# Selective-scan layer with routed experts: packed small TensorE products, a reordered chunk border, and fewer C products on VectorE

## Time and profile before

| | us |
|---|---|
| median of 3 runs | 815.91 |
| lowest and highest | 810.96 and 816.17 |
| the profiled execution's own time | 810.87 |
| its span, first to last instruction | 808.9 |
| mean granted TensorE clock (1 is full) | 0.939 |
| PE, DVE, POOL, ACT busy | 717.3, 525.1, 514.4, 482.0 |

### The profile page before, as it was taken

One profiled execution on the slowest core, in us unless ns is written; L12 is line 12 of the kernel. 1 busy time (PEld: TensorE's weight loads), 2 busy tenths in 40 slices (PEclk: granted clock), 3 DMA queues, 4 the chain that ended last, 5 costly groups with the idle time before them and its releaser, 6 DMA issues. The chain is left out here.

```text
span 808.9 us, 17785 instructions
## 1 busy us (share of the span) xinstructions
PE 717.3 (89%) x5898; PEld 626.9 (78%) x5899; DVE 525.1 (65%) x901; ACT 482.0 (60%) x977; POOL 514.4 (64%) x641
## 2 busy tenths in 40 slices
PE   7689899899998997898898875969999999999993
PEld 6567778677777776777676875958999999999992
DVE  4778989988889899779699973353333343333430
ACT  3579899899898986877886662412322333223320
POOL 1499789788887996998998763642333443334420
PEclk9589999999999997989999987979999999999997
DMA  9677843253243433634555659421111111111000
GB/s 217 179 227 260 285 131 108 90 133 105 79 133 105 118 92 82 113 76 107 113 92 62 170 157 259 37 19 62 56 43 60 38 40 53 42 55 50 25 8 1
DMA packets 45768, 82.58 MB, mean 102 GB/s; under 512 B 7800, under 2 KB 16253, under 8 KB 45696
## 3 DMA queue, kind: packets, MB, share of 16 engines
q1 hardware_dynamic: 39680, 69.05, 32.1%
q0 software_dynamic: 6016, 12.61, 6.3%
HBM read 70.48 MB, written 13.91 MB: 104 GB/s over the span
## 5 line engine op out<-in xcount | busy, mean ns | idle before, releaser
L618 POOL TENSOR_TENSOR w_sb<-w_sb,Csb 128x512 f32<-128x512 f32 x218 | 275.9, 1275 | 56.1 <-DVE w_sb L1151 53.6
L1151 DVE TENSOR_TENSOR_SCAN w_sb<-WW,hlast,w_sb 128x512 f32<-128x512 f32 x164 | 202.3, 1268 | 26.9 <-PE WW L974 19.7
L855 ACT ACTIVATE dt<-WW,b1c 128x128 f32<-128x128 f32 x312 | 89.1, 370 | 194.1 <-PE WW L1050 184.4
L959 PEld LDWEIGHTS WW<-b_sb,xin 64*128 64x128 f32 x2048 | 133.7, 198 | 76.0 <-issue 50.1
L959 PE MATMUL WW<-b_sb,xin 64*128 64x130 f32 (+1 forms) x2048 | 159.0, 297 | 37.4 <-DVE w_sb L1151 22.9
L784 ACT ACTIVATE w_sb<-dt,negA 128x512 f32<-128x512 f32 x256 | 170.1, 709 | 12.7 <-DVE dt L1180 7.4
L1066 PE MATMUL misc<-w_sb,dt 128*128 x624 | 144.1, 385 | 8.7 <-issue 8.3
L990 PE MATMUL YY<-sm,w_sb 128*128 128x128 f32 x1024 | 146.3, 290 | 0.0
L678 POOL DMA_INDIRECT y_out<-CbX,ocol x39 | 44.7, 1147 | 153.9 <-DVE CbX L1462 153.6
L1066 PEld LDWEIGHTS misc<-w_sb,dt 128*128 128x128 f32 x624 | 117.8, 194 | 24.1 <-issue 9.2
L990 PEld LDWEIGHTS YY<-sm,w_sb 128*128 128x128 f32 x1024 | 129.7, 160 | 0.0
(11 more groups left out here) (213 smaller groups left out, 821.9 us busy)
## 6 DMA issues: line engine op xcount, KB each, us to landing
w_sb<-c_rows SPq DMA_DIRECT2D x86, 256.0 KB
CbX<-c_rows SPq DMA_DIRECT2D x42, 256.0 KB, 3.9
w_sb<-w_in SPq DMA_DIRECT2D x20, 512.0 KB, 5.9
token_rows<-row SPq DMA_DIRECT2D x16, 512.0 KB
w_sb<-w_in SPq DMA_DIRECT2D x24, 256.0 KB
xin<-x_in SPq DMA_DIRECT2D x16, 256.0 KB, 4.1
w_sb<-x_in SPq DMA_DIRECT2D x14, 256.0 KB, 9.4
b_sb<-b_in SPq DMA_DIRECT2D x1, 780.0 KB, 6.4
```

The costliest lines, as they stand in the source:

```text
L618: eng.tensor_tensor(by_time(hc[g % NHC]), in_tiles(hb_of(g)), in_tiles(Csb[i % NCS][:, :]), ALU.mult).then_inc(s_hcp, 1)
L855: g = eng.activation(hT[u % 2][:, j * P:(j + 1) * P], hps[u % 2][:, j * P:(j + 1) * P], ACT.Gelu, bias=b1c[u][:, j:j + 1])
L959: return eng.matmul(to[:, at:at + width], x_rows[rows, k, h * P:(h + 1) * P], band[rows, k, at % P:at % P + width], start=(k == 0), stop=( ...
L1151: eng.tensor_tensor_scan(hb_of(g) if pooled(g) else w_of(g), w_of(g), A[g % NA], hlast[(q - 1) % 2][:, h * N + n:h * N + n + 1] if q % NC ...
```

## The change

- `VECTOR_UNITS`: (4, 10) in chunk 0, (8,) in chunks 1 to 6, (1, 5, 9, 13) in chunk 7. Seven pairs of items, 14 items, move from VectorE to GpSimd and ScalarE (19 pairs before, 12 after).
- cbt becomes one transpose of all four row tiles, spread over partition groups of 32 (CS = 32), instead of four; the four products of u read those groups, two at step 13 (`u_a`) and two at 14; its table is repeated in the four groups (made from a transpose of `invA4` and one VectorE instruction in the opening, ahead of the first `dt_add`, in place of two ScalarE copies).
- route becomes `routeT`: eight products with the 32-wide padded Wr stationary, each row tile into its own group of 32 PSUM partitions, then an evacuation (ScalarE) and one transpose a step later.
- bcd is split over two steps; xn0 and xn1 come one step earlier, vlast goes from 15 to 10, `row_products` from GpSimd's step 14 to 9.
- At the border (n = 0, 1) `add_y` comes ahead of `make_w`; `finish_rows`, `ln2_stats` and `aggregate` come one item earlier; `dt_add` and `u_times_x` move by one item or less.
- `choose(1)` and rank of chunks 4 to 6 leave chunk 7 and go behind the last scan; the routing of chunk 7 is done ahead of `outputs(0)`; `choose(2)` goes to tile 0, `place_tokens(2)` to tile 1; twelve `enlist` DMAs go out at tile 0 in a row.

The core of the diff (left out: constants, the wiring of buffers and semaphores in the opening, `u_times_x` and `logits` reading the new places, the evacuations, and the host's padded arrays):

```diff
@@ -27,7 +27,7 @@
 ITEMS = N * KD
-VECTOR_UNITS = [(1, 6, 11)] + [(1, 9)] * 6 + [(1, 5, 9, 13)]
+VECTOR_UNITS = [(4, 10)] + [(8,)] * 6 + [(1, 5, 9, 13)]
...
@@ -63,30 +64,33 @@
-LATE = (("xnr0", NQ - 1), ("xnr1", NQ - 1), ("route", NQ - 1), ("rank", NQ - 1), ("lists", 1))
+PARTS = ("bcd_a", "u_a")
+LATE = (("xnr0", NQ - 1), ("xnr1", NQ - 1), ("routeT", NQ - 1), ("route", NQ - 1), ("rank", NQ - 1), ("lists", 1))
 def hops(q):
     if q + 1 < NQ:
-        at = {1: ("cbt", q), 3: ("xn0", q + 1), 4: ("xn1", q + 1), 5: ("bcd", q + 1), 6: ("brow", q + 1),
-              7: ("dt2_0", q + 1), 10: ("dt2_1", q + 1), 13: ("u01", q), 14: ("u23", q), 15: ("vlast", q + 1)}
+        at = {1: [("cbt", q)], 2: [("xn0", q + 1)], 3: [("xn1", q + 1)], 4: [("bcd_a", q + 1)], 5: [("bcd", q + 1)],
+              6: [("brow", q + 1)], 7: [("dt2_0", q + 1)], 10: [("dt2_1", q + 1), ("vlast", q + 1)], 13: [("u_a", q)],
+              14: [("u01", q), ("u23", q)]}
         if q:
-            at |= {8: ("xnr0", q - 1), 9: ("xnr1", q - 1), 11: ("route", q - 1)}
+            at |= {8: [("xnr0", q - 1)], 9: [("xnr1", q - 1)], 11: [("routeT", q - 1)], 12: [("route", q - 1)]}
         if q == BATCHES[0][1] + 1:
-            at |= {0: ("rank", BATCHES[0][1] - 1)}
+            at |= {0: [("rank", BATCHES[0][1] - 1)]}
     else:
-        at = {1: ("cbt", q), 3: ("u01", q), 4: ("u23", q), 6: ("lists", 0), 8: ("xnr0", q - 1), 9: ("xnr1", q - 1),
-              10: ("route", q - 1), 13: ("turn", 0), 15: ("rank", 6)}
+        at = {1: [("cbt", q)], 3: [("u_a", q)], 4: [("u01", q), ("u23", q)], 6: [("lists", 0)],
+              8: [("xnr0", q - 1)], 9: [("xnr1", q - 1)], 10: [("routeT", q - 1)], 11: [("route", q - 1)],
+              13: [("turn", 0)]}
     return at
-TAIL = LATE
+TAIL = (("rank", BATCHES[1][1] - 1),) + LATE
...
@@ -639,7 +649,7 @@
                         make_hc(KD * m)
                     if first and 1 <= n < NQ:
                         rstd_ahead(n)
-                    if n == 14 and not last:
+                    if n == 9 and not last:
                         row_products(q + 1, 1 - b)
                     if n == 5 and not first:
...
@@ -697,12 +707,10 @@
                     b1_copy(t + 3, (u + 3) % 4)
                 if isinstance(t, int) and t == 0:
                     rstd(1, NQ)
-                if isinstance(t, int) and t < 3:
-                    if t == 0:
-                        eng.wait_ge(s_lists, 16)
-                    enlist(1, range(16 + 4 * t, 20 + 4 * t))
+                    eng.wait_ge(s_lists, 16)
+                    enlist(1, range(16, 28))
                 put(t, u)
-                if isinstance(t, int) and t == 2:
+                if isinstance(t, int) and t == 1:
                     enlist(2, range(28, NT))
...
@@ -870,15 +872,32 @@
         @block.tensor
         def _(eng):
+            def u_product(k, q):
+                at = spot("u23" if k % 2 else "u01", q)[:, k // 2 * D:(k // 2 + 1) * D]
+                return eng.matmul(at, cbt[CS * k:CS * k + N + 1, :], table_of_u[CS * k:CS * k + N + 1, :],
+                                  start=True, stop=True)
             def fill(name, q):
-                b, to, before = q % B, spot(name, q), BEFORE[name, q]
-                if before:
+                b = q % B
+                if name == "u_a":
+                    wait_read(eng, *BEFORE["u01", q])
+                    wait_read(eng, *BEFORE["u23", q])
+                    if q == NQ - 1:
+                        eng.wait_ge(s_first, 1)
+                    wait_read(eng, "cbt", q)
+                    for k in range(2):
+                        mm = u_product(k, q)
+                    mm.then_inc(s_ua, 1)
+                    return
+                part_of = {"bcd_a": "bcd"}.get(name, name)
+                to, before = spot(part_of, q), BEFORE[part_of, q]
+                if before and name not in ("bcd", "u01", "u23"):
                     wait_read(eng, *before)
...
-                if name == "u01" and q == NQ - 1:
-                    eng.wait_ge(s_first, 1)
...
-                elif name == "bcd":
-                    wait_read(eng, "xn1", q)
-                    for h in range(KD):
-                        mm = eng.matmul(to[0:CBD, :], col("wcd", h * CBD, (h + 1) * CBD), xnT[h],
-                                        start=(h == 0), stop=(h == KD - 1))
+                elif name in ("bcd_a", "bcd"):
+                    h = int(name == "bcd")
+                    wait_read(eng, f"xn{h}", q)
+                    mm = eng.matmul(to[0:CBD, :], col("wcd", h * CBD, (h + 1) * CBD), xnT[h],
+                                    start=(h == 0), stop=(h == KD - 1))
+                    if h == 0:
+                        return
                 elif name == "brow":
                     wait_read(eng, "bcd", q)
...
@@ -908,25 +929,24 @@
                                         start=True, stop=True)
                 elif name == "cbt":
                     eng.wait_ge(s_cb, 2 * q + 1)
-                    for i in range(TI):
-                        mm = eng.transpose(to[0:N + 1, i * P:(i + 1) * P], cbrow[:, i, :], ident)
+                    mm = eng.transpose(to[:, 0:P], cbrow[:, :, :].rearrange("p i n -> p (i n)"), ident)
                 elif name in ("u01", "u23"):
-                    wait_read(eng, "cbt", q)
-                    for i in range(2):
-                        k = i + (2 if name == "u23" else 0)
-                        mm = eng.matmul(to[:, i * D:(i + 1) * D], cbt[:, k * P:(k + 1) * P],
-                                        table_of_u[0:N + 1, :], start=True, stop=True)
+                    eng.wait_ge(s_ua, q + 1)
+                    mm = u_product(2 + int(name == "u23"), q)
...
                 elif name == "route":
+                    wait_read(eng, "routeT", q)
+                    mm = eng.transpose(to[:, 0:P], routed, ident)
+                elif name == "routeT":
                     wait_read(eng, "xnr1", q)
-                    for i in range(TI):
-                        for h in range(KD):
-                            mm = eng.matmul(to[:, i * E:(i + 1) * E], xnrT[h][:, i * P:(i + 1) * P],
-                                            col("wr", h * E, (h + 1) * E), start=(h == 0), stop=(h == KD - 1))
+                    for h in range(KD):
+                        for i in range(TI):
+                            mm = eng.matmul(to[CS * i:CS * (i + 1), 0:P], col("wr", h * CS, (h + 1) * CS),
+                                            xnrT[h][:, i * P:(i + 1) * P], start=(h == 0), stop=(h == KD - 1))
                 elif name == "rank":
                     batch = READ[name, q][1] - 1
...
@@ -995,13 +1017,16 @@
                 at = hops(q)
                 for n in range(N):
                     m = N * q + n
-                    if n in at:
-                        fill(*at[n])
-                    make_w(m + 2)
+                    for hop in at.get(n, ()):
+                        fill(*hop)
+                    if n > 1:
+                        make_w(m + 2)
                     add_y(KD * m - 4)
                     add_y(KD * m - 3)
-            eng.wait_ge(s_pconst, 6)
+                    if n < 2:
+                        make_w(m + 2)
...
@@ -1077,14 +1103,11 @@
                     hidden(t + 1, (u + 1) % 4)
                 if not (isinstance(t, int) and t + 2 >= MT):
                     turn_x(t + 2, (u + 2) % 4, r + (u + 2) // 4)
+                if isinstance(t, int) and t == 0:
+                    for hop in TAIL[0:5]:
+                        fill(*hop)
+                outputs(t, u)
                 if isinstance(t, int) and t == 1:
-                    fill("xnr1", NQ - 1)
-                outputs(t, u)
-                if isinstance(t, int) and t == 0:
-                    fill("xnr0", NQ - 1)
-                if isinstance(t, int) and t == 1:
-                    fill("route", NQ - 1)
-                if isinstance(t, int) and t == 2:
                     fill("rank", NQ - 1)
                 if isinstance(t, int) and t == 4:
                     fill("lists", 1)
...
@@ -1332,28 +1359,26 @@
                 def between(j, gap):
                     if not first:
-                        if (j, gap) in ((4, 1), (5, 1)):
-                            finish_rows(q - 1, j - 4)
-                        if (j, gap) in ((6, 1), (7, 1)):
-                            ln2_stats(j - 6, q - 1)
-                        if (j, gap) == (8, 1):
+                        if (j, gap) in ((3, 1), (4, 1)):
+                            finish_rows(q - 1, j - 3)
+                        if (j, gap) in ((5, 1), (6, 1)):
+                            ln2_stats(j - 5, q - 1)
+                        if (j, gap) == (7, 1):
                             aggregate(1, q - 1)
                         if (j, gap) == ((24, 0) if last else (26, 0)):
                             logits(q - 1)
-                    if not last and (j, gap) in ((20, 0), (27, 0)):
```

(36 more changed lines are left out.)

77 lines of the change are left out of this document (45 added, 32 removed).

## The result

The changed kernel takes 822.18 us (median of 4 runs, 821.32 to 823.36), the kernel before beside it 813.43 (4 runs, 810.3 to 816.17). The ratio is 1.0112, 95% interval 1.0079 to 1.0145. The profiled execution took 823.36 with a span of 821.6; before it was 810.87 and 808.9.

What follows compares the result with a forecast made beforehand. No engine was full in middle chunks; GpSimd bound chunks 5 and 6, TensorE's chain the tail. −11.4 to the last scan and −9.3 for the tail gave 790.2, or 795.2 from the runs' median; it said 794, range 780 to 811.

Steps and rivals of the forecast that it cites:

- I cost it at nothing: Border, TensorE's xn0 waiting for the normed x: covered by VectorE's finishing and statistics; bare, up to 1.5 a chunk.
- I take 2.0: Chunks 1 to 3: idle left on top of GpSimd's 49.5, making 51.5 for chunks 1 and 2; −7.8 over three.
- Chunk 0, +0.5: Chunk 0: GpSimd takes 2.6 more product work, 59.4 busy with 3.5 idle, 62.9 in all.
- Chunk 4, −4: Chunk 4: routing's serial steps no longer have a C pair beside them on VectorE, 58.02 to 54.0.
- Chunk 5, −0.3: Chunk 5: GpSimd 52.99 + 2.6 with 3 idle, 58.6 in all.
- Chunk 6, +2: Chunk 6: GpSimd 57.07 + 2.6 with 3 idle, 62.7 in all.
- Chunk 7, −2.3: Chunk 7: `choose(1)` leaves four places between the last scans; its pairs stay.
- Opening, +0.5: Opening: one more VectorE instruction, 0.44, ahead of the first `dt_add`, on the way to the first exponential.
- Tail, −9.3: Behind the last scan: hops, routing waits and table work leave the first tiles; estimated between 3 and 14.
- Hops on TensorE, 1.85 saved: Each middle chunk: cbt saves 0.45, u products 0.8, route 0.6, together 1.85 of TensorE's 49.8.
- Rival 1: GpSimd's 7.3 idle is structural, so chunks 0 to 6 cost 2.6 more each: 823, chance 0.10.
- Rival 3: A new wait, at xn0 or a hop, replaces those removed; chunks 1 to 3 stay at 54: 805, chance 0.17.

Runs made afterwards that it cites:

- h2: The kernel before with xn0 at step 2 and xn1 at step 3, all else as it was: 812.63 us, ratio 1.0003.
- e1: The changed kernel with VectorE's pairs of C products put back to three in chunk 0 and two in chunks 1 to 6: 813.53 us, ratio 1.0004.
- e3: The changed kernel with xn0 and xn1 back at steps 3 and 4 and both halves of bcd at step 5: 813.11 us, ratio 1.0009.
- e2: The kernel before with only the new choice of pairs, two in chunk 0 and one in chunks 1 to 6: 814.33 us, ratio 1.0002.
- g1: The changed kernel with xn0, xn1, bcd, dt_add put back, three pairs in chunk 0, two in chunk 6, u at step 3 in chunk 7: 802.81 us.
- h1: The changed kernel with only chunk 0 put back to three pairs on VectorE, at 1, 6 and 11: 818.4 us, ratio 1.0059.
- f2: The changed kernel with xn0, xn1 back at steps 3 and 4, both bcd halves at 5, dt_add behind scans 20 and 27: 805.52 us, ratio 0.9918.
- h3: The kernel before with dt_add moved to the early places, scans 19 and 25 instead of 20 and 27: 810.64 us, ratio 0.9983.
- e4: The changed kernel with dt_add back behind scans 20 and 27: 813.31 us, ratio 0.9998.
- g2: As g1, but three pairs instead of two on VectorE in chunk 6: 799.89 us, ratio 0.984 against the kernel before.
- i1: As g2, with xnr0, xnr1, routeT and route of the last chunk behind outputs of tile 0, rank still ahead: 799.67 us, ratio 0.9857.

## Why the prediction was wrong

The sign was wrong, and 822.2 lies above the range. By its steps:

- **"I cost it at nothing", xn0 at step 2: the step that failed.** It named the wait and said it would be up to 1.5 a chunk bare. It was 3.5 a chunk, and beside it the stretch of half clock in the middle chunks was 6.8 long instead of 3.4. The cover named, VectorE's finishing and statistics, shrank by edits that were summed as gains: TensorE is free for xn0 2.3 sooner than in h2, 1.4 of it by the pair (e1), and the norm is done some 0.7 later. Undone together with the split of bcd (e3), it gives 8.6 us.
- **`dt_add` was not costed at all.** The forecast walked through hops and border and left out two instructions that the diff moves by half an item and an item and a half (the list of the change says one item or less). In their new places they wait for a logarithm on ScalarE, 3.0 a chunk, and 1.9 with the old pairs (e1), where ScalarE has two copies fewer. Undone, they give 8.4 us.
- **"I take 2.0" of idle on top of GpSimd's 49.5.** In the changed kernel 5.9; without the two waits 3.3 in chunk 1 and 52.2 to 52.9 a chunk, 4.5 less than before for three chunks instead of 7.8. So even the clean figure was 1.1 a chunk too low.
- **Chunk 0, +0.5: measured +8.0.** The 2.6 of product work was right, but the wrong duration was asked for. GpSimd has power operations for seven chunks beside its first items. That the old pair at unit 1 let it keep up is likely, but not separated from the number of pairs. Pairs alone cost 3.7 in the kernel before (e2), and going back to three saves 4.9 (g1) and 6.5 (h1).
- **Chunk 4, −4: measured +1.6**, and 0.0 in f2. The forecast let its serial steps shrink with the C pair; why they did not, no run shows. **Chunk 5, −0.3: −3.4** in the profiles; the kernel before had a clock of 0.86 there and the changed one 0.94, and h2, with the old pairs, takes 58.4 too. The gain is mostly a slow chunk 5 in the one profile that was forecast from. **Chunk 6, +2: +4.3**, the term whose profiles scatter most (60.7 and 65.5 for one kernel). **Chunk 7, −2.3: +1.5**, and −1.2 in f2. Its profiles scatter too: the chunk 7 of before takes 58.0, 62.4 in e2, 57.9 in h2 and 60.2 in h3. So what `choose(1)` took with it can't be read from them.
- **Opening, +0.5: +2.7** in this profile. The added instruction is 0.45. The rest is not the change's: with the same opening e4 scans from 31.4 on and g2 from 34.7, and the two kernels h2 and h3, whose opening is that of before, from 29.1 and 33.1.
- **Tail, −9.3: −5.1**, and −8.0 in f2. The pieces named went (hops, tables, the 9.1), and the price of "0 to 2" for the routing chain was 2.9 (i1). But the 326.5 that it was forecast from were those of one long tail: e2, h2 and h3, whose tail is that of before, take 324.2, 322.8 and 323.3, and 44.4, 44.9 and 43.9 instead of 49.0 from tile 0 to tile 4. Against these the changed kernel's tail gains about 2 and that of f2 about 5.
- **Hops on TensorE, 1.85 saved: more was saved** (route 1.85 to 0.65, u 1.12 to 0.70): in chunk 3 TensorE is busy 47.54 in f2 and 49.78 in the kernel before, at the same granted clock of 0.97. The saving of 0.6 for route should have been 1.1, its transpose taken off. No run has the old hops in the changed kernel, so what the saving is worth in time is not shown. The Trainium skill, TensorE: Matmul & The Clock Gate, Measured speedup vs the span model, has 2.38 times for three column groups; here four take 2.8 times less.
- **The rivals.** Rival 1 had the number, 823, but its mechanism is not what happened: it needed 7.3 of idle and periods above 56, and the idle time went when the waits went. Rival 3 had the mechanism, a wait at xn0, but only one of the two waits, chunks 1 to 3 left at 54 where they took 55.1, and no cost in chunk 0. (The rivals' times are counted from 815.9, the forecast of 794 from between 810.9 and 815.9; no verdict hangs on it.)

## What to carry to other kernels

When several edits go in together, price every moved instruction in the kernel that they make, not in the one before: two moves that cost nothing in the kernel before (h2, h3) cost 8 us each in the changed one, and giving the work back to VectorE (e1) removes only a third of either wait. Walk through every line of the diff that moves an instruction past its producer's time, not only those that move much. And choose a division of shared work by stretch: in these profiles one pair did for VectorE in the middle chunks, and three were better than two in the first. And read a stretch in several executions before it is forecast from: chunk 5 and the tail of the one profile used here were 2 to 4 us longer than in others with the same code there.
